# Spreading a per-batch preparation over two steps of a TensorE-bound kernel

## The reference

```python
# attention part, per batch
q, k1, k2, v1, v2 = (x + x @ W.T + b for the five W, b)     # split into heads
S1 = k1^T v1 / n;  S2 = k2^T v2 / n                          # 8x8 per head
S12 = S1 * S2
out = (q @ S1) * mean(v2) * g1 + S12.sum(2) * g2 + (q @ S2) * mean(v1) * g3 + (q @ S12) * g4
out = layernorm(out) * ln_g + ln_b
a = out @ Wo.T + bo
x1 = layernorm(x + a)
# feed-forward part: only expert 0 has weight
f = relu(x1 @ w1[0] + b1[0]) @ w2[0] + b2[0]
y3 = layernorm(x1 + f) * gamma + beta
result = layernorm(x1 + y3)
```

## Time and profile before

| | us |
|---|---|
| median of 3 runs | 203.22 (203.04 to 203.26) |
| profiled execution | 202.93 |
| its span, first to last instruction | 201.2 |
| TensorE matmuls busy | 190.6 (95%) |
| VectorE busy | 156.9 (78%) |
| GpSimd busy | 141.6 (70%) |
| ScalarE busy | 129.1 (64%) |

### The profile page before, as it was taken

The page is one execution under the profiler, slowest core; times in us unless marked ns, Lnnn a source line. Parts: engine busy times, 40 slices in busy tenths (PEclk is TensorE's granted clock), DMA queues, the critical chain, the costliest instruction groups (busy, mean ns, idle before and its releaser), DMA issues.

```text
span 201.2 us, 4296 instructions
## 1 busy us (share of the span) xinstructions
PE 190.6 (95%) x1369; PEld 174.4 (87%) x1369; DVE 156.9 (78%) x470; ACT 129.1 (64%) x386; POOL 141.6 (70%) x191
## 2 busy tenths in 40 slices
PE   6999999999999999999999999999999999999930
PEld 6898979999898989999997989898989899988820
DVE  0286717988879796988879896989698969897683
ACT  0433456553859565975768685867597759786852
POOL 8627490675599838984698859985998598876450
PEclk9999999999999999999999999999999999999985
DMA  5999502000001100101010300110010101010012
GB/s 169 199 285 286 134 0 82 3 2 3 0 3 49 55 2 0 57 0 52 3 52 28 104 3 0 54 53 4 0 52 5 52 3 52 2 52 30 25 54 104
DMA packets 12641, 10.64 MB, mean 53 GB/s; under 512 B 730, under 2 KB 10475, under 8 KB 12619
## 3 DMA queue, kind: packets, MB, share of 16 engines
q1 hardware_dynamic: 11960, 9.32, 15.0%
q0 software_dynamic: 352, 0.92, 2.2%
q10 hardware_dynamic: 306, 0.13, 0.2%
HBM read 6.17 MB, written 4.20 MB: 52 GB/s over the span
## 4 chain that ended last, share of the span: by engine, by line
PE 86%; DVE 6%; issue 3%; POOL 2%; ACT 1%; DVEq 0%; POOLq 0%
PE down_ps L1045 25%; PE up_ps L1045 25%; PE z_ps L1045 14%; PE prep_ps L1045 13%; PE turn_ps L1204 3%; PE turn_ps L1175 3%; DVE st L814 1%; DVE down_ps L865 1%; POOL y2g L567 1%; POOL y L571 1%; DVE z_ps L925 1%; ACT res L690 1%; DVE y2n L821 1%; PE z_ps L1055 0%; DVE res L1022 0%
## 5 line engine op out<-in xcount | busy, mean ns | idle before, releaser
L1045 PE MATMUL down_ps<-w_sb,hT 128*128 128x128 f32 x480 | 58.9, 276 | 0.1
L1045 PEld LDWEIGHTS down_ps<-w_sb,hT 128*128 128x128 f32 x480 | 56.4, 192 | 0.7 <-ACT hT L708 0.3
L708 ACT ACTIVATE hT<-up_ps,cols 128x512 f32<-128x512 f32 x64 | 42.2, 682 | 5.2 <-PE up_ps L1045 5.0
L690 ACT ACTIVATE res<-y,nb,rstd 128x128 f32<-128x128 f32 x60 | 24.8, 483 | 6.6 <-POOL nb L535 5.9
L595 POOL TENSOR_TENSOR x1b<-x,b_rows 128x512 f32<-128x512 f32 x16 | 20.6, 1286 | 10.4 <-DVE x L821 10.4
L1045 PE MATMUL up_ps<-x1T_hi,w_hi 128*128 128x512 f32 x64 | 26.1, 408 | 0.0
L1045 PE MATMUL up_ps<-x1T_lo,w_hi 128*128 128x512 f32 x64 | 25.4, 398 | 0.0
L1045 PE MATMUL up_ps<-x1T_hi,w_lo 128*128 128x512 f32 x64 | 25.3, 395 | 0.0
L567 POOL TENSOR_TENSOR y2g<-y2n,gamma_rows 128x512 f32<-128x512 f32 x15 | 19.2, 1282 | 4.8 <-DVE y2n L821 4.8
L821 DVE TENSOR_SCALAR x<-z_ps,st,rstd 128x128 f32<-128x128 f32 x64 | 21.9, 404 | 0.1
L657 ACT ACTIVATE z_sq<-z_ps 128x128 f32<-128x128 f32 x64 | 16.8, 270 | 7.7 <-PE z_ps L1045 7.7
(11 more groups left out here) (170 smaller groups left out, 417.0 us busy)
## 6 DMA issues: line engine op xcount, KB each, us to landing
out<-res SPq DMA_DIRECT2D x15, 256.0 KB, 2.0
X<-in_L_attn_x SPq DMA_DIRECT2D x7, 512.0 KB, 8.7
V_all<-V_dram SPq DMA_DIRECT2D x6, 128.0 KB, 3.0
X<-in_L_attn_x SPq DMA_DIRECT2D x2, 256.0 KB, 3.5
w_sb<-in_L_ffn_w POOLq DMA_DIRECT2D x2, 256.0 KB, 7.8
out<-res SPq DMA_DIRECT2D x2, 128.0 KB, 2.2
w_raw<-in_L_attn_Wv ACTq DMA_DIRECT2D x2, 64.0 KB, 2.3
w_raw<-in_L_attn_Wk SPq DMA_DIRECT2D x2, 64.0 KB, 3.2
```

The lines of the kernel that those rows point to most:

```text
L690: last = act.activation(res[buf][:, t, :], y3[buf][:, t, :], ACT.Identity, scale=rstd4[:, t:t + 1], bias=nb4[:, t:t + 1])
L708: act.activation(hT[:, k, :], up_ps[k % len(up_ps)][:, :], ACT.Relu, bias=cols[:, 5 + k:6 + k]).then_inc(relu_out, 1)
L1045: return pe.matmul(o, lhsT, rhs, start=start, stop=stop)
```

## The change

For batches 2 to 7 the preparation is spread over two steps. G·A, E, A_k·E and S move to the odd step before (1, 3, ..., 11): `gram_av` in that step's product, E within its y2n, `ak_e` after the whole of `up`, `s_out` after x1. The even step keeps GpSimd's `prepare`, then `attention_matrix` directly after `up` and ahead of the turning of x, `PT_copy` ahead of the high half of xT on ScalarE, and `centered` ahead of `down`'s third tile. `centered` for these batches takes six passes of split operands (PT_hi, PT_lo, both_hi, both_lo) in place of two fp32 matmuls; VectorE makes PT_lo (`PT_rest`) after the low half of xT, GpSimd splits `center` once in step 0. `split_G` moves from the end of GpSimd's even step to between xu and x1b. The V rows of batches 5 to 7 move from step 7 to step 6.

At the start the warming matmuls read a matrix of ones that VectorE sets, and there are seven; two more tiles of batch 2's Gram product stand ahead of product 0. At the end VectorE does group 14's y3 by itself (`y2d_before`, `y3_before`), ScalarE's last Relu is in halves, and the order of VectorE's and ScalarE's last operations changes.

```diff
@@ Step
-                self.v_set = {0: 0, 7: 1}.get(n)
-                self.v_rest = {0: 0, 7: 1}.get(n)
+                self.pre = n % 2 == 1 and n > 0 and self.seq(3) < BATCHES
+                self.v_set = {0: 0, 6: 1}.get(n)
+                self.v_rest = {0: 0, 6: 1}.get(n)
+            def early(self):
+                return self.seq(3)
@@ SP, store
-                    if (b, g) in ((0, 0), (2, 1)):
+                    if (b, g) in ((0, 0), (2, 0)):
@@ GpSimd
+            def split_both():
+                pool.wait_ge(zw_ready, 1)
+                pool.tensor_copy(both_hi[:, :, :], center[:, :, :]).then_inc(both_split, 1)
+                pool.wait_ge(both_split, 1)
+                pool.tensor_tensor(both_lo[:, :, :], center[:, :, :], both_hi[:, :, :].bitcast(f32), ALU.subtract).then_inc(both_split, 1)
...
                 if st.n == 0:
                     split_A()
+                    split_both()
...
-                if st.prev:
+                if st.prev and not st.last:
...
+                if st.cur and n % 2 == 0 and n // 2 + 2 < BATCHES:
+                    split_G(n // 2 + 2)
...
-                if st.cur and n % 2 == 0 and n // 2 + 2 < BATCHES:
-                    split_G(n // 2 + 2)
@@ ScalarE
-                act.activation(PT_sb[:, :], prep_ps[:, 0:XW], ACT.Copy).then_inc(PT_out, 1)
+                act.activation(PT_sb[:, :] if b < 2 else PT_hi[:, :], prep_ps[:, 0:XW], ACT.Copy).then_inc(PT_out, 1)
...
-                    relu(st, 3)
+                    if st.last:
+                        for h in range(2):
+                            relu_half(st, 3, h)
+                    else:
+                        relu(st, 3)
+                if st.prep and st.n >= 0:
+                    PT_copy(st.prepared())
                 if st.nxt2 and st.n >= 0:
                     xT_upper(n + 2)
...
+            root4(GROUPS - 2)
             half_std(st3, std3, 0, end_st3, end_std3)
...
-            root4(GROUPS - 2)
@@ VectorE
+            dve.memset(warm_in[:, :], 1.0).then_inc(warm_set, 1)
...
+            def PT_rest(b):
+                wait(dve, PT_out, b + 1)
+                dve.tensor_tensor(PT_lo[:, :], prep_ps[:, 0:XW], PT_hi[:, :].bitcast(f32), ALU.subtract).then_inc(PTlo_out, 1)
+            def y2d_before(m):
+                wait(dve, sq_out, GROUPS * TILES)
+                wait(dve, std1_out, GROUPS)
+                wait(dve, st3_out, m + 1)
+                for t in range(TILES):
+                    last = dve.scalar_tensor_tensor(out=y2d[:, t, :], in0=y2_tile(t),
+                                                    scalar=st3[:, t // 2, 3 * (t % 2) + 1:3 * (t % 2) + 2],
+                                                    in1=gamma_rows[:, :], op0=ALU.subtract, op1=ALU.mult)
+                last.then_inc(y2d_out, 1)
+            def y3_before(m, buf):
+                dve.wait_ge(y2d_out, 1)
+                wait(dve, x1beta_out, m + 1)
+                wait(dve, res_out, m - 1)
+                for t in range(TILES):
+                    last = dve.scalar_tensor_tensor(out=y3[buf][:, t, :], in0=y2d[:, t, :],
+                                                    scalar=rstd3[:, t:t + 1], in1=x1beta[buf][:, t, :],
+                                                    op0=ALU.mult, op1=ALU.add)
+                last.then_inc(y3_last, 1)
...
+                if st.last:
+                    y2d_before(n - 1)
...
+                if st.last:
+                    y3_before(n - 1, (s - 1) % 2)
+                if st.prev and not st.last:
                     wait(dve, y2g_out, n - 1)
-                    normalize(y2n, y2_tile, st3, rstd3, y2n_out, (lambda: e_and_v(st.prepared())) if st.prep else None)
+                    normalize(y2n, y2_tile, st3, rstd3, y2n_out, (lambda: e_and_v(st.early())) if st.pre else None)
...
-                if st.prep and st.n >= 0:
-                    s_out(dve, st.prepared())
...
                     xT_rest(n + 2)
+                if st.prep and st.n >= 0:
+                    PT_rest(st.prepared())
...
                     PQ_rest(st.ready)
+                if st.pre:
+                    s_out(dve, st.early())
...
+            y3_stats(GROUPS - 2, 1 - own)
             half_y2(0)
+            result_factors(GROUPS - 2)
+            result_bias_here(GROUPS - 2)
             half_r3(0)
...
-            y3_stats(GROUPS - 2, 1 - own)
             half_y2(1)
             y2d_second()
-            result_factors(GROUPS - 2)
-            result_bias_here(GROUPS - 2)
@@ TensorE
+                    pe.wait_ge(S_out, b - EARLY + 3)
...
-                    wait(pe, G_out, min(BATCHES, b + 4))
+                    wait(pe, G_out, min(BATCHES, b + 3))
...
+                if b >= 2:
+                    wait(pe, PTlo_out, b - 1)
+                    pe.wait_ge(both_split, 2)
+                    hi, lo = (t[:, :, :].rearrange("p j c -> p (j c)") for t in (both_hi, both_lo))
+                    for part, pt in ((slice(0, 256), lambda t: t[:, 0:C]),
+                                     (slice(256, 512), lambda t: t[:, C:C + 1].to_broadcast([128, 128]))):
+                        mm(prep_ps[:, part], pt(PT_hi), hi, start=True, stop=False)
+                        mm(prep_ps[:, part], pt(PT_hi), lo, start=False, stop=False)
+                        last = mm(prep_ps[:, part], pt(PT_lo), hi, start=False, stop=True)
+                    last.then_inc(p_done, 1)
+                    return
...
+                    pe.wait_ge(warm_set, 1)
+                    keep_warm(7)
                     pe.wait_ge(consts, 1)
-                    keep_warm(6)
...
-                    gram(2, range(2, 4))
+                    gram(2, range(2, 6))
...
-                    product(n + 1, st.seq(1), (lambda: gram_av(st.prepared())) if st.prep else None)
+                    product(n + 1, st.seq(1), (lambda: gram_av(st.early())) if st.pre else None)
...
-                if st.prep:
-                    ak_e(st.prepared())
...
                     up(n, 3)
+                if st.pre:
+                    ak_e(st.early())
+                if st.prep:
+                    attention_matrix(st.prepared())
...
-                        if t == 2 and st.prep:
-                            attention_matrix(st.prepared())
                         for k in range(FCH):
-                            if t == 2 and k == 2 and st.prep:
+                            if t == 2 and k == 0 and st.prep:
                                 centered(st.prepared())
```

More of the change, by code:

```diff
@@ L105, in build @@
         warm = sb("warm", [128, 1])
+        warm_in = sb("warm_in", [128, 128])
         minus = sb("minus", [128, TILES])
@@ L123, in build @@
         PT_sb = sb("PT_sb", [128, XW])
+        PT_hi = sb("PT_hi", [128, XW], f32r)
+        PT_lo = sb("PT_lo", [128, XW], f32r)
+        both_hi = sb("both_hi", [128, 2, 128], f32r)
+        both_lo = sb("both_lo", [128, 2, 128], f32r)
         PQ_hi = sb("PQ_hi", [128, 512], f32r)
@@ L192, in build @@
         const_set = sem("const_set")
+        warm_set = sem("warm_set")
         consts = sem("consts")
@@ L233, in build @@
         rows_done = sem("rows_done")
+        both_split = sem("both_split")
+        PTlo_out = sem("PTlo_out")
         A_split = sem("A_split")
@@ L257, in build @@
         res_out = sem("res_out")
+        y2d_out = sem("y2d_out")
+        y3_last = sem("y3_last")
         end_y2 = sem("end_y2")
@@ L604, in _ @@
             pool.wait_ge(end_y2n, 1)
-            pool.wait_ge(y3_out, GROUPS - 1)
+            pool.wait_ge(y3_out, GROUPS - 2)
             pool.tensor_tensor(y2g[:, 0:2, :], y2n[:, 0:2, :], rows(gamma_rows[:, :], 2), ALU.mult).then_inc(end_y2g, 1)
@@ L708, in relu, with relu_half @@
                 act.activation(hT[:, k, :], up_ps[k % len(up_ps)][:, :], ACT.Relu, bias=cols[:, 5 + k:6 + k]).then_inc(relu_out, 1)
+            def relu_half(st, k, h):
+                part = slice(h * GROUP // 2, (h + 1) * GROUP // 2)
+                wait(act, up_done, st.n * FCH + (k + 1))
+                act.activation(hT[:, k, part], up_ps[k % len(up_ps)][:, part], ACT.Relu,
+                               bias=cols[:, 5 + k:6 + k]).then_inc(relu_out, 1)
             def body(st):
@@ L744, in body @@
                     root4(n - 2)
-                if st.prep:
+                if st.prep and st.n < 0:
                     PT_copy(st.prepared())
@@ L770, in half_std @@
                                bias=eps_col[:, :], scale=1.0 / C).then_inc(done, 1)
+            root4(GROUPS - 2)
             half_std(st3, std3, 0, end_st3, end_std3)
             act.wait_ge(end_nb, 1)
-            act.wait_ge(y2g_out, GROUPS - 1)
+            act.wait_ge(y2g_out, GROUPS - 2)
             for t in range(2):
@@ L843, in y3_stats @@
             def y3_stats(m, buf):
-                wait(dve, y3_out, m + 1)
+                if m == GROUPS - 2:
+                    dve.wait_ge(y3_last, 1)
+                else:
+                    wait(dve, y3_out, m + 1)
```

(18 more changed lines are left out.)

## The result

The changed kernel took 209.56 us (median of 4, 209.45 to 210.13) beside 203.13 for the kernel before on the same chip: 3.25% slower, ratio 1.0325 with a 95% interval of 1.0288 to 1.0363. I had written 201.7 and 0.91 for faster. The profiled execution took 209.45, its span 207.7.

What follows compares the result with a forecast made beforehand. TensorE's own work and its waits were taken to bound the kernel. Start -0.10, pairs with Gram products -0.72, pairs without +0.15, end -0.85: -1.5 us from the 203.22 median, 201.7; 8-in-10 range 199.4 to 202.7.

Steps and rivals of the forecast that it cites:

- The split of G stands before x1b in even steps ... hidden, by 0.3.: GpSimd's even steps: the added 0.8 split delays y2g and y3 to 7.2, while mr waits for 7.5 anyway; no cost.
- M's wait: Steps 8, 10, 12: M ready at 5.4, TensorE asks at 4.70, waits 0.75; bounds 0.4 and 1.1.
- pairs without a Gram product: Steps 7 to 12, three pairs: 20.98 each against 20.94 before, +0.15 in all.
- The centered product: Six times on TensorE: six split passes take 0.71 in place of fp32's 0.95, gain 0.24 each; bounds nothing and 0.24.
- Just in time: 0 taken, 0.1 a step possible: P's low half on VectorE: ready at 7.2, TensorE asks at 7.27, so no wait counted.
- dear passes: Rival: the centered product's passes cost what fp32 did, 6 x 0.24 back, 203.1, no change; chance 0.04.
- In time by 0.1; 0 taken: Gram product's wait for VectorE's S: S ready at 9.4, TensorE there at 9.5, so no cost.
- pairs with a Gram product: Steps 1 to 6, three pairs: the centered product's gain with no new wait, 22.0 each, -0.72 in all.
- The end: Last operations: statistics at 195.05 against 195.91, -0.85; bounds -0.3 and -1.1.
- The sign that I had named: At the end: the statistics would come 0.85 nearer to the last matmuls.
- The start: Earlier warming matmuls may end TensorE's slow rate sooner: -0.1, bounds 0 and -0.3; two more Gram tiles bring 0.

Runs made afterwards that it cites:

- e1: The changed kernel with G's split directly behind GpSimd's preparation, ahead of mr; 202.62 us, ratio 0.9997 to the kernel before.
- e2: The changed kernel with mr and nb behind y3 in even steps too, G's split left in place; 202.78 us, ratio 1.0003.
- e5: e1 with GpSimd's x1beta of steps 1, 3, ..., 11 left to the next step, behind prepare; 199.50 us, ratio 0.9839.
- e8: e1 with attention matrix and centered product later on TensorE, ScalarE's copy of P behind xT's high half; 199.75 us, ratio 0.9853.
- e4: e1 with the centered product of batches 2 to 7 in two fp32 matmuls as before, no low half of P; 202.68 us, ratio 1.0.
- e6: e5 with the centered product of batches 2 to 7 in fp32; 199.69 us, ratio 0.9857.
- e10: e5 with S on VectorE ahead of xT's low half in place of behind x1; 198.96 us, ratio 0.9797.
- e3: The kernel before with the change's start and end, the middle untouched; 201.85 us, ratio 0.9963.
- e9: e5 with the start of the kernel before: six warming matmuls on the identity matrix, two Gram tiles back behind product 0; 199.85 us, ratio 0.9836.
- e11: e5 run once more, unchanged, as the measure for e9 and e10; 199.25 us, ratio 0.9822.

## Why the prediction was wrong

**The step that failed: "The split of G stands before x1b in even steps ... hidden, by 0.3."** I followed this edit forward on its own engine, to what it delays there (x1beta, y2g, y3, mr), found 0.3 of cover and stopped. I did not ask who reads its output. That reader is the split Gram product, and the same change had moved it from the even step into the odd one, where the halves made in the step before are needed at once. All numbers were in my text: mr 8.1, nb, y2g, y3 and xu to 12.3, split to 13.1 in the even step's count; the odd step began at 11.0, and TensorE asks after two tiles, 11.95. A wait of 1.15. Measured 1.10 to 1.16, in steps 3, 5, 7, 9 and 11 (the halves for step 1 are made in step 0, where GpSimd is idle). e1 and e2 show this from two sides.

**Its price.** This much waiting costs about 1.4 a pair: the changed kernel's pairs are 1.36, 1.40, 1.37, 1.47 and 1.37 longer than e1's, 7.0 in sum, the timing gives 6.7. The 0.59 of the three passes after the wait, 0.36 without it, is 0.23 of the difference.

**M's wait.** Right in place, steps and size: 0.75 forecast, 0.76 seen (0.71 to 0.74 in e1), none in steps 2, 4 and 6. What I left out is the restart: e5 puts the price at 0.97 for the pair. So pairs without a Gram product took 21.25 in e1, not 20.98. It did eat all that the middle gained.

**The centered product.** Forecast 0.24 a batch, from 0.95 to 0.71. The piece went to 0.80. The size of the passes was right: with P's low half in time they take 0.69 to 0.71 (e8). What I had wrong was on both sides of the difference. The 0.95 held a wait of 0.09 for ScalarE's copy of P, which I read as work (0.86 without it, e4); and the term "Just in time: 0 taken, 0.1 a step possible" for P's low half came out at its 0.1, in all six steps. So the passes by themselves bring 0.06 in the chain, 0.05 by pairs (e5 against e6), where by these pieces they would bring 0.16, my estimate, with P's low half in time. The waits are read from the traces; e8 moves two other pieces as well, and no run takes P's low half away alone. Rival "dear passes" put the time at 203.1, near what e1 measured, but by luck: what e1 lost, it lost to the restart and to S.

**S ahead of the Gram products.** I wrote "In time by 0.1; 0 taken". It was late by 0.16, three times (e10). In pairs with a Gram product this eats most of what else was gained: 22.21 in e1 against 22.26 before, where I had 22.0. Without this wait they take 22.05 and 22.02 (e10).

**The end.** Forecast -0.85, measured -0.76 in the trace of the changed kernel, -0.73 in that of e3. The sign that I had named came out at half its size: the end's statistics begin 2.76 after the last matmuls in place of 3.22, 0.46 nearer and not 0.85; 0.21 came ahead of the end of those matmuls and 0.09 behind the statistics. One thing was not in my count: of VectorE's two last y3 operations the first was long in the changed kernel,

```profile
201.50 0.96 DVE L1077 SCALAR_TENSOR_TENSOR y<-z_sq,rstd,x1beta 128x128 f32<-128x128 f32 x2
```

701 ns and 341 ns, where before the two took 348 on average. GpSimd's y ran at the same time (its timeline):

```profile
201.34 0.72 POOL L632 TENSOR_TENSOR y<-y2g,x1beta 128x256 f32<-128x256 f32 x1
```

It ended at 202.06, and VectorE's first operation at 202.2. The Trainium skill, "SBUF — State Buffer", section "SBUF: two separate sides", says that a VectorE operation with two SBUF inputs and a GpSimd operation lock one port pair against each other for a whole instruction. The two rows agree with it. So do the other runs: in all twelve traces with the new end the two operations take 0.96 together while GpSimd's 0.72 runs; in the kernel before GpSimd's ended at 195.01, ahead of VectorE's first at 195.26, and the two take 0.61. No run moves one of them alone.

**The start.** The trace of the changed kernel has x's first turning at 9.21 against 9.78, but e1 has 9.54, e4 9.97 with the same start, and e9 9.62 with the old one. What differs most is TensorE's rate: the four transposes of the weights took 0.44 in the changed kernel's execution and 0.89 in the one before, with a granted clock of 1.00 in the windows of both kernels. A term of 0.1 cannot be read from one execution; e9 against e11 gives 0.3 by the ratios, with intervals that overlap. What the start brings stays open.

**The sum with G's wait taken out.** e1 is the change as I had forecast it. Its ratio of 0.9997 puts it at 203.2 beside the median of 203.22, 1.5 over my 201.7. The mis-sized terms make that up: 0.27 a pair after M's wait (21.25 for 20.98), nearly all of it the restart, 0.8 in three; 0.2 a pair where there is a Gram product, 0.16 to 0.18 of it the wait for S, 0.6; 0.1 at the end. The rest of the 209.56 is G's wait.

## What to carry to other kernels

When a change moves a consumer to an earlier step, walk back through every input of it to the queue that makes it, and compare the moment of need with the moment of readiness. It is not enough to follow each moved producer forward on its own engine. An operation that waits (here a 0.2 us one for the last normalization) sets the time of all behind it in its queue, so what another engine needs soon goes ahead of it; moving two operations, 0.7 us together, was worth 6.7 us here. Before a piece is taken as the price of an operation, see whether its weight load begins right behind the end of what it reads: 0.09 of the 0.95 here was a wait that no view of waits listed. And add the restart to a wait: 0.74 of standing cost 0.97.

## What the runs showed of the hardware

TensorE's first pieces after a wait are longer than the same pieces in the run of work: the attention matrix 0.61 after waiting for M and 0.34 without, the split Gram product 0.59 after waiting for G_lo and 0.36 without. In the run of work the attention matrix's weight load begins 0.22 ahead of its first matmul (117.97 and 118.19 in e5); after the wait both begin at 123.10. Six or seven warming matmuls, of two records each, did not fix when TensorE's early matmuls become twice as fast: 0.44 to 0.89 for the same four transposes in different executions, and the granted clock, 1.00 in the first windows of both kernels, does not show it. And a VectorE operation with two SBUF inputs took 701 ns beside one of GpSimd; the next of its kind, when GpSimd's had ended, took 341.
